# Key transfers of an attention kernel issued from ScalarE's queue instead of SyncE's

## The chip, the core and the metric

The kernel runs on one core of a Trainium2 chip. The time is the device time of one execution in microseconds (us). The core has five engines, each of which takes its own instructions in order: PE (TensorE), DVE (VectorE), ACT (ScalarE), POOL (GpSimd) and SP (SyncE, which here only issues transfers). They meet at semaphores. 16 DMA engines do the transfers; an engine's queue only issues them.

## The reference

Eight images of 32 x 32 tokens go through one transformer layer of width 128: an embedding with a position table, causal attention with 8 heads of 16, and a feed-forward block with a shared and 8 routed experts of which each token takes 2. Cut to what matters here:

```python
h = x @ W + pe                                    # (8, 1024, 128)
z = layernorm(h)
Q, K, V = (split_heads(z @ w + b) for w, b in ((Wq, bq), (Wk, bk), (Wv, bv)))
attn = softmax((Q @ K.T + causal_mask) / sqrt(16))
h = h + (attn @ V) @ Wo + bo
f = layernorm_with_scale(layernorm(h))
h = h + shared_expert(f) + sum_over_top2(weight[e] * expert[e](f))
```

Everything is float32. The products that need it are made of three passes with split operands: a high part (`_h`) and the rest (`_l`).

## The kernel before, in words

An image has 1024 tokens, worked on in two halves of 512. Its heads are taken in two groups of four, so the attention has four units, a group and a half of the queries each. For an image the steps are, in their names in the code: `emb`, `turn1`, `q`, `k`, `v` for each half (embedding, normalisation, transposed tokens, the two projections and the values); 64 `score` steps, first pass, which find the largest score of every query; 96 `prob` steps in 24 groups of four, second pass, in which PE makes transposed scores in one of two banks, ACT takes their exponential into `pt`, and `weigh` multiplies by the values; then the projection (`to`, `ant`, `oproj`), the second normalisation, routing (`gates`, `route`), and the feed-forward steps `in`, `expert`, `shared`, `counts` and `combine`.

**The stacks.** Both passes of scores multiply `q_stack` by `k_stack`. In each, three copies of a head's 16 rows lie below each other (high, high, low for the queries; high, low, high for the keys), with the even heads' copies in partitions 0 to 47 and the odd heads' from partition 64. The copies are made by DMA within the core's memory: six transfers of 128 KB for the queries of a half and six for its keys. What is copied are `qk_h`, which ACT writes straight from the projection (L953), and `qk_l`, which POOL subtracts (L1101). `stack_in[half]` counts the twelve transfers; PE waits for all of them before `score 0` of an image (half 0) and before `score 32` (half 1).

**Order.** A table (`PERIOD`) lists all steps of one period in one order, and every engine walks through it and does its own part of each step. In a period the second pass and the feed-forward part of image i are woven with the front (`emb` to `v`) and the first half of the scores of image i+1. `FIRST` is the same front for image 0, and `LAST` is the rest for image 7, so seven periods hold a front of a next image. The keys of half 0 may be overwritten once the last probability step that reads them is through (`KEYS_USED`, the 20th group of 24); until then SP's `keys` waits. All transfers of the loop are issued by SP.

Since each engine takes its instructions in order, an instruction that waits, or one that takes long to issue, holds everything behind it on that engine.

Of the kernel before, what the change touches and what calls it, by code (L numbers as in the profile page):

```python
# [36 lines left out]
P = 128  # L37
# [4 lines left out]
HEADS, DH = 8, 16  # L42
G4 = 4
# [7 lines left out]
ODD = 64  # L51
# [12 lines left out]
NS, NP_, NU = len(SCORE_STEPS), len(PROB_STEPS), len(UNITS)  # L64
# [3 lines left out]
KEYS_USED = max(k for k, (_, kt) in enumerate(PROB_STEPS) if kt < HT)  # L68
# [10 lines left out]
def later(i):  # L79

    return not (isinstance(i, int) and i == 0)
# [15 lines left out]
def of_next_image(st):  # L97

    return (st[0] in ("emb", "turn1", "q", "k", "v") or st[0] == "score" and st[1] < 2 * UNIT_S or
            st[0] == "turn" and st[1] < 2)  # L100
# [49 lines left out]
PERIOD = period(WEAVE, streams())  # L150
# [14 lines left out]
def build(nc, x_t, tok_w, pos, wq, wk, wv, wo, bq, bk, bv, bo, ln_s, ln_b, w_in, w_shared, w_expert, w_bias,  # L165
          w_gate, b_gate, out):
    with ExitStack() as ctx:
# [3 lines left out]
        def sem(name):  # L171
            return ctx.enter_context(nc.semaphore(name))
# [36 lines left out]
        qk_h, qk_l = sb("qk_h", [P, 2, S], F32R), sb("qk_l", [P, 2, S], F32R)  # L209
        v = sb("v", [P, TILES, HEADS, VW])  # L210

        q_stack = sb("q_stack", [P, 2, HEADS, HALF], F32R)
        k_stack = sb("k_stack", [P, HEADS // 2, S], F32R)
# [55 lines left out]
        front_mm = sem("front_mm")  # L269
# [9 lines left out]
        qkh_made, qkl_made = sem("qkh_made"), sem("qkl_made")  # L279
        v_made = sem("v_made")  # L280
        stack_in = [sem(f"stack_in_{half}") for half in range(2)]
# [4 lines left out]
        st_ready, exp_done, mask_done = sem("st_ready"), sem("exp_done"), sem("mask_done")  # L286
# [18 lines left out]
        stacks_zeroed = sem("stacks_zeroed")  # L305
# [4 lines left out]
        def halfs(half):  # L310
            return slice(half * HALF, (half + 1) * HALF)
# [4 lines left out]
        def front_step(i, what, half):  # L316

            return i * NF + FRONT_STEPS.index((what, half)) + 1
# [5 lines left out]
        def words(ap):  # L324

            return ap.bitcast(F32)
# [4 lines left out]
        @block.sync  # L331
        def _(sp):
            def load_x(i):
                sp.dma_start(x_sb[:], x_t[:, bass.ds(i * S, S)]).then_inc(x_in, 16)

            load_x(0)
            for dst, src in ((tokw_sb, tok_w), (pos_sb, pos)):
                sp.dma_start(dst[:], src).then_inc(w_in0, 16)
            for dst, src in ((wq_sb, wq), (wk_sb, wk), (bq_sb, bq), (bk_sb, bk),
                             (wv_sb, wv), (bv_sb, bv), (bo_sb, bo)):  # L340
                sp.dma_start(dst[:], src).then_inc(w_in1, 16)
            for dst, src in ((wo_sb, wo), (lns_sb, ln_s), (lnb_sb, ln_b), (win_sb, w_in), (wshared_sb, w_shared),
                             (wex_sb, w_expert), (wbias_sb, w_bias), (wgate_sb, w_gate), (bgate_sb, b_gate)):
                sp.dma_start(dst if dst is win_sb or dst is wex_sb else dst[:], src).then_inc(w_in2, 16)

            sp.wait_ge(const_made, CONSTS)
            sp.wait_ge(stacks_zeroed, 3)
            for n in range(HEADS // 2):
                sp.dma_start(words(k_stack[SHIFT:P, n, :]), words(minus1.rearrange("r c n -> r (c n)"))).then_inc(ones_in, 16)

            def stacks(i, half, w):

                if w == 0:
                    sp.wait_ge(qkh_made, i * 4 + 2 * half + 2)
                    sp.wait_ge(qkl_made, i * 4 + 2 * half + 2)
                for n, part in enumerate((qk_h, (qk_h, qk_l)[w], (qk_l, qk_h)[w])):
                    for odd in range(2):
                        to = slice(odd * ODD + n * DH, odd * ODD + (n + 1) * DH)
                        stack = k_stack[to, :, halfs(half)] if w else q_stack[to, half, odd::2, :]
                        rows = part[odd * (P // 2):(odd + 1) * (P // 2), w, halfs(half)]  # L360
                        sp.dma_start(words(stack), words(rows)).then_inc(stack_in[half], 16)  # L361

            def maxima(i, u):

                g, half = UNITS[u]
                sp.wait_ge(ml_made, i * NU + u + 1)
                for row, part in ((SHIFT, mrow_h), (SHIFT + 1, mrow_l)):
                    dst = q_stack[row:row + 1, half, g * G4:(g + 1) * G4, :]
                    sp.dma_start(words(dst), words(part[:, u, :])).then_inc(m_in[u], 16)

            def store(i, half):
                sp.wait_ge(ex_step, (i * TILES + (half + 1) * HT) * COMBINE)
                sp.dma_start(out_v[i, :, tiles(half), :], acc[:, tiles(half), :]).then_inc(out_done[half], 16)

            def stage(i, st, loads=True):
                if st[0] == "turn":
                    maxima(i, st[1])
                elif st == ("k", 0):
                    stacks(i, 0, 0)
                    if not later(i):  # L380
                        stacks(i, 0, 1)
                elif st == ("k", 1):
                    stacks(i, 1, 0)
                    stacks(i, 1, 1)
                    if loads:
                        load_x(i + 1)
                elif st == ("combine", 3):
                    store(i, 0)
                elif st == ("combine", 7):
                    store(i, 1)  # L390

            def keys(i):

                sp.wait_ge(exp_done, i * NP_ * G4 + (KEYS_USED + 1) * G4)
                stacks(i + 1, 0, 1)

            def image(i, loads):
                for n, st in enumerate(PERIOD):
                    stage(i + of_next_image(st), st, loads)
                    if n == max(PERIOD.index(("k", 0)), PERIOD.index(("prob", KEYS_USED, G4 - 1))):  # L400
                        keys(i)

            for st in FIRST:
                stage(0, st)
            image(0, True)
            for i in range(1, B - 2):
                image(i, True)
            image(B - 2, False)
            for st in LAST:
                stage(B - 1, st)  # L410
            for half in range(2):
                sp.wait_ge(out_done[half], B * 16)
# [525 lines left out]
        def _(act):  # L938
            def front(i, kind, half):
                if kind == "turn1":  # L940
                    if later(i):
                        act.wait_ge(z2l_made, i * 2 - 1 + half)
                    act.wait_ge(front_mm, front_step(i, "turn1", half))
                    src = (b7, b6)[half]
                    nc.scalar.copy(zt[:, halfs(half)], src[:]).then_inc(zt_made, 1)
                    nc.scalar.copy(zt_h[:, halfs(half)], src[:]).then_inc(zth_made, 1)
                if kind in ("q", "k"):
                    w = "qk".index(kind)
                    src, bias = (b6 if half and w else b7), (bq_sb, bk_sb)[w]
                    act.wait_ge(front_mm, front_step(i, kind, half))  # L950
                    nc.scalar.activation(qk[:, w, halfs(half)], src[:], ACT.Identity,
                                         bias=bias[:, 0:1]).then_inc(qk_made, 1)
                    nc.scalar.activation(qk_h[:, w, halfs(half)], src[:], ACT.Identity,  # L953
                                         bias=bias[:, 0:1]).then_inc(qkh_made, 1)

            def take(i, u):

                g, half = UNITS[u]
                act.wait_ge(pv_done, i * NP_ + UNIT_LAST[u] + 1)
                nc.scalar.copy(ot[:, g, halfs(half)], b6[:]).then_inc(pv_taken, 1)  # L960
# [69 lines left out]
            def stage(i, st):  # L1030
                if st[0] == "prob":
                    prob(i, st[1], st[2])
                elif st[0] == "take":
                    take(i, st[1])
                elif st[0] in ("turn1", "q", "k"):
                    front(i, st[0], st[1])
                elif st[0] in ("in", "counts", "expert", "combine"):
                    forward(i, st)
                elif st[0] in ("ant", "z2t", "route"):
                    post(i, st)  # L1040

            def image(i):
                for st in PERIOD:
                    stage(i + of_next_image(st), st)

            act.wait_ge(w_in1, 7 * 16)
            for st in FIRST:
                stage(0, st)
            act.wait_ge(w_in2, 9 * 16)
            nc.scalar.copy(win_h[:], win_sb).then_inc(wsplit_h, 1)  # L1050
            nc.scalar.copy(wex_h[:], wex_sb).then_inc(wsplit_h, 1)
# [189 lines left out]
```

## Time and profile before

| | |
|---|---|
| Time, 3 runs | 1180.1 us median (1179.13 to 1182.12) |
| The profiled execution | 1181.4 us, its span 1179.6 us |
| PE busy | 1063.7 us, 90% of the span |
| DVE / ACT / POOL busy | 64% / 53% / 33% |
| Granted TensorE clock, mean | 0.938 of full speed |
| Share of PE in the chain that ended last | 75% |
| Share of the transfers and SP's issues in that chain | 6% and 5% |

A period takes about 139.9 us: the last key transfer of half 0 was issued at 430.75 us in one and at 570.64 us in the next. The times of a row are microseconds from the start of the span. "Idle before" is the time in which the engine had nothing to execute, with the instruction that ended it. In the views by stretch, PEclk 1.00 is the full TensorE clock of 2.4 GHz and 0.50 is 1.2 GHz; a value between them means that the clock changed within the stretch.

### The profile page before, as it was taken

The page shows a single profiled execution, that of the slowest core. Times are in us where ns is not written, and L with a number is a line of the kernel's source. Part 1 is how long each engine was busy: PE and PEld are TensorE (multiplying, and loading weights), DVE is VectorE, ACT ScalarE, POOL GpSimd, SP SyncE. Part 2 cuts the span into 40 slices and gives each one's busy share as a digit, 9 for nine tenths or more (in the row PEclk, how much of TensorE's full clock was granted, in tenths as well). Part 3 has the DMA queues.
Part 4 walks back from the last instruction along what each step waited for, and adds up shares of the span by engine and source line. Part 5 has one row for each costly group of instructions (what it writes and reads, how often), then busy time and mean ns, then how long its engine had stood idle before and what let it go on. Part 6 is the DMA issues. An engine that isn't in the chain of part 4 may idle for free.

```text
span 1179.6 us, 16622 instructions
## 1 busy us (share of the span) xinstructions
PE 1063.7 (90%) x5632; PEld 706.6 (60%) x5632; DVE 756.8 (64%) x2118; ACT 628.9 (53%) x1395; POOL 388.0 (33%) x514
## 2 busy tenths in 40 slices
PE   2589988999799988999889998899979998899997
PEld 1345566556675566755666556755667556675575
DVE  3387558874678537785387755787377854778444
ACT  1226825567346654567345672556734665446743
POOL 5321424313432234412353142432333223441233
PEclk9969988999899998999889998899989999899999
DMA  3530032103040040400404003310304004040000
GB/s 96 70 43 1 16 40 50 29 2 48 8 67 11 2 54 10 68 1 2 54 20 58 2 17 39 54 24 1 51 8 64 11 2 54 10 64 1 1 1 18
DMA packets 28547, 34.60 MB, mean 29 GB/s; under 512 B 5402, under 2 KB 15552, under 8 KB 28336
## 3 DMA queue, kind: packets, MB, share of 16 engines
q1 hardware_dynamic: 28464, 33.55, 18.3%
q8 instruction: 45, 0.74, 0.3%
q14 instruction: 38, 0.31, 0.1%
HBM read 3.61 MB, written 4.19 MB: 7 GB/s over the span
## 4 chain that ended last, share of the span: by engine, by line
PE 75%; DVE 7%; DMA 6%; SPq 5%; ACT 4%; issue 2%; POOL 1%; DVEq 0%; POOLq 0%; ACTq 0%
PE bank L517 15%; PE bank L536 12%; PE pair L488 9%; PE bank L488 5%; DMA k_stack<-qk_h 5%; PE pair L656 5%; PE pair L657 5%; PE pair L658 5%; SPq L361 5%; ACT pt L969 2%; PE pair L419 2%; PE pair L420 2%; PE pair L421 2%; PE bank L637 2%; PE bank L431 1%
## 5 line engine op out<-in xcount | busy, mean ns | idle before, releaser
L969 ACT ACTIVATE pt<-bank 128x512 f32<-128x512 f32 (+3 forms) x768 | 346.6, 493 | 211.6 <-PE bank L517 204.3
L741 DVE CUSTOM_DVE_ANT_0 pair<-pair,causal 128x640 f32<-128x640 f32 (+3 forms) x256 | 257.2, 1047 | 36.9 <-PE pair L488 34.8
L517 PE MATMUL bank<-q_stack,k_stack 128*128 128x512 f32 (+2 forms) x768 | 266.2, 399 | 9.2 <-ACT pt L969 7.3
L517 PEld LDWEIGHTS bank<-q_stack,k_stack 128*128 128x128 f32 x768 | 135.6, 190 | 165.1 <-ACT pt L969 126.3
L1113 POOL TENSOR_SCALAR_AFFINE_SELECT pt<-pt 128x512 f32<-128x512 f32 x128 | 81.7, 638 | 364.5 <-ACT pt L969 364.5
L536 PE MATMUL bank<-pt,v 128*32 128x512 f32 (+3 forms) x1536 | 168.9, 513 | 2.1 <-ACT pt L969 2.1
L741 DVE CUSTOM_DVE_ANT_0 bank<-bank,causal 128x128 f32<-128x128 f32 (+3 forms) x256 | 121.9, 509 | 61.1 <-PE bank L488 60.7
L488 PE MATMUL pair<-k_stack,q_stack 112*128 112x512 f32 (+2 forms) x512 | 148.8, 380 | 7.4 <-issue 6.2
L488 PE MATMUL bank<-k_stack,q_stack 112*128 112x256 f32 (+2 forms) x256 | 90.1, 424 | 29.1 <-DMA k_stack<-qk_h 22.7
L488 PEld LDWEIGHTS pair<-k_stack,q_stack 112*128 112x128 f32 x512 | 86.2, 191 | 44.8 <-DVE mx L741 28.8
L656 PE MATMUL pair<-wex_h,hid_h 128*128 128x512 f32 x256 | 106.9, 418 | 0.6 <-POOL hid_l L1136 0.4
L1015 ACT ACTIVATE from_act<-pair,gm 128x512 f32<-128x512 f32 x64 | 44.1, 689 | 113.3 <-PE pair L658 105.0
L657 PE MATMUL pair<-wex_l,hid_h 128*128 128x512 f32 x256 | 104.4, 408 | 0.0
L658 PE MATMUL pair<-wex_h,hid_l 128*128 128x512 f32 x256 | 104.1, 407 | 0.0
L1144 POOL TENSOR_TENSOR from_dve<-from_act 128x256 f32<-128x256 f32 x64 | 46.7, 730 | 171.9 <-ACT from_act L1021 171.2
L1021 ACT ACTIVATE from_act<-from_dve,wsel 128x128 f32<-128x128 f32 x256 | 81.7, 391 | 35.9 <-DVE from_dve L893 35.4
L488 PEld LDWEIGHTS bank<-k_stack,q_stack 112*128 112x128 f32 x256 | 52.3, 228 | 50.5 <-DMA k_stack<-qk_h 26.5
L893 DVE SCALAR_TENSOR_TENSOR from_dve<-pair,gm,from_act 128x512 f32<-128x512 f32 x64 | 47.8, 747 | 50.9 <-PE pair L658 47.5
L866 DVE SCALAR_TENSOR_TENSOR from_dve<-from_act,pair 128x512 f32<-128x512 f32 x64 | 43.9, 685 | 47.4 <-PE pair L421 43.9
L741 DVE DVE_READ_ACCUMULATOR2_ANT mx<- 128x1 f32 x512 | 72.2, 141 | 0.0
L419 PE MATMUL pair<-z2t_h,win_h 128*128 128x512 f32 x128 | 59.1, 462 | 2.0 <-issue 1.8
L658 PEld LDWEIGHTS pair<-wex_h,hid_l 128*128 128x128 f32 x256 | 50.2, 196 | 12.6
(142 smaller groups left out, 1537.6 us busy)
## 6 DMA issues: line engine op xcount, KB each, us to landing
q_stack<-qk_h SPq DMA_DIRECT2D x64, 128.0 KB, 4.0
k_stack<-qk_h SPq DMA_DIRECT2D x64, 128.0 KB, 6.5
q_stack<-qk_l SPq DMA_DIRECT2D x32, 128.0 KB, 5.0
k_stack<-qk_l SPq DMA_DIRECT2D x32, 128.0 KB, 6.7
out<-h SPq DMA_DIRECT2D x16, 256.0 KB, 2.3
pt<-w_expert SPq DMA_DIRECT2D x1, 1024.0 KB
x_sb<-x_t SPq DMA_DIRECT2D x8, 116.0 KB
pos_sb<-pos SPq DMA_DIRECT2D x1, 512.0 KB
```

The costliest lines, as they stand in the source:

```text
L361: sp.dma_start(words(stack), words(rows)).then_inc(stack_in[half], 16)
L419: nc.tensor.matmul(dst, wh, xh, start=first, stop=False)
L488: mm = nc.tensor.matmul(dst[:, a:b], q_stack[0:STACK, t // HT, hd, t % HT * P:(t % HT + 1) * P], k_stack[0:STACK, hd // 2, a:b], start=Tru ...
L517: nc.tensor.matmul((b4, b5)[p % 2][:, c0:HALF], k_stack[:, hd // 2, kt * P:(kt + 1) * P], q_stack[:, half, hd, c0:HALF], start=True, stop= ...
L536: mm = nc.tensor.matmul(b6[32 * j:32 * j + VW, q0:HALF], v[:, kt, g * G4 + j, :], pt[:, k % PT_SLOTS, j, q0:HALF], start=(kt == 0), stop=( ...
L656: nc.tensor.matmul(dst, hid_h[:, c, tok], wex_h[:, c, w], start=(c == 0), stop=False)
L657: nc.tensor.matmul(dst, hid_h[:, c, tok], wex_l[:, c, w], start=False, stop=False)
L658: mm = nc.tensor.matmul(dst, hid_l[:, c, tok], wex_h[:, c, w], start=False, stop=(c == HID // P - 1))
L741: nc.vector.tensor_tensor_reduce(src, src, causal[:, S - n:S], 1.0, -3.0e38, ALU.add, ALU.max, mx[:, col:col + 1]).then_inc(s_taken, 1)
L969: nc.scalar.activation(pt[:, k % PT_SLOTS, j, q0:HALF], (b4, b5)[p % 2][:, q0:HALF], ACT.Exp, scale=0.25).then_inc(exp_done, 1)
L1021: nc.scalar.mul(from_act[:, t % 2, part], from_dve[:, t % 2, part], wsel[:, t, e:e + 1]).then_inc(weighted, 1)
L1113: nc.gpsimd.affine_select(out=d, in_=d, compare_op=ALU.is_ge, fill=0.0, base=0, pattern=[[0, G4], [1, P]], channel_multiplier=-1).then_inc ...
```

## The change

The six transfers of the keys of a half move from SP's queue to ACT's. On SP stay those of the queries, and their wait changes: they no longer wait for the keys' parts to be made, only for the queries' own. On ACT a function `keys` waits for the keys' parts (both of ACT's and POOL's), and for image 1 and later also until PE is through with the keys that are overwritten, then issues six transfers. For half 0 that stands after the step at place 161 of the table (`in 3`, second part), for half 1 in the step `("v", 1)`, which ACT had nothing to do in. SP's load of the next image's tokens gets a wait of its own. The diff, whole:

```diff
--- before.py
+++ after.py
@@ -348,17 +348,17 @@
             for n in range(HEADS // 2):
                 sp.dma_start(words(k_stack[SHIFT:P, n, :]), words(minus1.rearrange("r c n -> r (c n)"))).then_inc(ones_in, 16)
 
-            def stacks(i, half, w):
-
-                if w == 0:
-                    sp.wait_ge(qkh_made, i * 4 + 2 * half + 2)
-                    sp.wait_ge(qkl_made, i * 4 + 2 * half + 2)
-                for n, part in enumerate((qk_h, (qk_h, qk_l)[w], (qk_l, qk_h)[w])):
+            def queries(i, half):
+
+                sp.wait_ge(qkh_made, i * 4 + 2 * half + 1)
+                sp.wait_ge(qkl_made, i * 4 + 2 * half + 1)
+                if half and later(i):
+                    sp.wait_ge(st_ready, i * NP_ * G4)
+                for n, part in enumerate((qk_h, qk_h, qk_l)):
                     for odd in range(2):
                         to = slice(odd * ODD + n * DH, odd * ODD + (n + 1) * DH)
-                        stack = k_stack[to, :, halfs(half)] if w else q_stack[to, half, odd::2, :]
-                        rows = part[odd * (P // 2):(odd + 1) * (P // 2), w, halfs(half)]
-                        sp.dma_start(words(stack), words(rows)).then_inc(stack_in[half], 16)
+                        rows = part[odd * (P // 2):(odd + 1) * (P // 2), 0, halfs(half)]
+                        sp.dma_start(words(q_stack[to, half, odd::2, :]), words(rows)).then_inc(stack_in[half], 16)
 
             def maxima(i, u):
 
@@ -376,29 +376,20 @@
                 if st[0] == "turn":
                     maxima(i, st[1])
                 elif st == ("k", 0):
-                    stacks(i, 0, 0)
-                    if not later(i):
-                        stacks(i, 0, 1)
+                    queries(i, 0)
                 elif st == ("k", 1):
-                    stacks(i, 1, 0)
-                    stacks(i, 1, 1)
+                    queries(i, 1)
                     if loads:
+                        sp.wait_ge(front_mm, front_step(i, "emb", 1))
                         load_x(i + 1)
                 elif st == ("combine", 3):
                     store(i, 0)
                 elif st == ("combine", 7):
                     store(i, 1)
 
-            def keys(i):
-
-                sp.wait_ge(exp_done, i * NP_ * G4 + (KEYS_USED + 1) * G4)
-                stacks(i + 1, 0, 1)
-
             def image(i, loads):
-                for n, st in enumerate(PERIOD):
+                for st in PERIOD:
                     stage(i + of_next_image(st), st, loads)
-                    if n == max(PERIOD.index(("k", 0)), PERIOD.index(("prob", KEYS_USED, G4 - 1))):
-                        keys(i)
 
             for st in FIRST:
                 stage(0, st)
@@ -953,6 +944,20 @@
                     nc.scalar.activation(qk_h[:, w, halfs(half)], src[:], ACT.Identity,
                                          bias=bias[:, 0:1]).then_inc(qkh_made, 1)
 
+            def keys(i, half):
+
+                act.wait_ge(qkh_made, i * 4 + 2 * half + 2)
+                act.wait_ge(qkl_made, i * 4 + 2 * half + 2)
+                if not later(i):
+                    act.wait_ge(stacks_zeroed, 3)
+                if later(i):
+                    act.wait_ge(st_ready, (i - 1) * NP_ * G4 + (NP_ if half else KEYS_USED + 1) * G4)
+                for n, part in enumerate((qk_h, qk_l, qk_h)):
+                    for odd in range(2):
+                        to = slice(odd * ODD + n * DH, odd * ODD + (n + 1) * DH)
+                        rows = part[odd * (P // 2):(odd + 1) * (P // 2), 1, halfs(half)]
+                        act.dma_start(words(k_stack[to, :, halfs(half)]), words(rows)).then_inc(stack_in[half], 16)
+
             def take(i, u):
 
                 g, half = UNITS[u]
@@ -1034,18 +1039,24 @@
                     take(i, st[1])
                 elif st[0] in ("turn1", "q", "k"):
                     front(i, st[0], st[1])
+                elif st == ("v", 1):
+                    keys(i, 1)
                 elif st[0] in ("in", "counts", "expert", "combine"):
                     forward(i, st)
                 elif st[0] in ("ant", "z2t", "route"):
                     post(i, st)
 
             def image(i):
-                for st in PERIOD:
+                for n, st in enumerate(PERIOD):
                     stage(i + of_next_image(st), st)
+                    if n == max(PERIOD.index(("k", 0)) + 6, PERIOD.index(("prob", KEYS_USED, G4 - 1))):
+                        keys(i + 1, 0)
 
             act.wait_ge(w_in1, 7 * 16)
             for st in FIRST:
                 stage(0, st)
+                if st == ("k", 0):
+                    keys(0, 0)
             act.wait_ge(w_in2, 9 * 16)
             nc.scalar.copy(win_h[:], win_sb).then_inc(wsplit_h, 1)
             nc.scalar.copy(wex_h[:], wex_sb).then_inc(wsplit_h, 1)
```

ACT's instructions in the first period around half 0, in the order of its program (an ACTIVATE of `pt` is the exponential of one probability step, `from_act<-pair` on L996 is the tanh of an `in` step, L1028 the copy of the counts; square brackets name the semaphores waited for). Before:

```order
L996 ACTIVATE from_act<-pair 128x512 [waits in_ready]
L969 ACTIVATE pt<-bank 128x512 [waits st_ready]
L969 ACTIVATE pt<-bank 128x384 [waits st_ready,pv_done]
L1004 CAST hid_h<-hid 128x512 [waits hid_made]
L996 ACTIVATE from_act<-pair 128x512 [waits in_ready]
L969 ACTIVATE pt<-bank 128x384 [waits st_ready] x2
L1028 COPY cnt_t<-bank 9x512 [waits cnt_ready]
L969 ACTIVATE pt<-bank 128x384 [waits st_ready]
```

After (the same instructions have other line numbers there: L996 is L1001, L969 is L974, L1004 is L1009, L1028 is L1033; L959 is the new issue):

```order
L1001 ACTIVATE from_act<-pair 128x512 [waits in_ready]
L974 ACTIVATE pt<-bank 128x512 [waits st_ready]
L974 ACTIVATE pt<-bank 128x384 [waits st_ready,pv_done]
L1009 CAST hid_h<-hid 128x512 [waits hid_made]
L1001 ACTIVATE from_act<-pair 128x512 [waits in_ready]
L959 DMA k_stack<-qk_h 16x4x512 [waits st_ready,qkl_made,qkh_made]
L959 DMA k_stack<-qk_h 16x4x512
L959 DMA k_stack<-qk_l 16x4x512 x2
L959 DMA k_stack<-qk_h 16x4x512 x2
L974 ACTIVATE pt<-bank 128x384 [waits st_ready] x2
L1033 COPY cnt_t<-bank 9x512 [waits cnt_ready]
L974 ACTIVATE pt<-bank 128x384 [waits st_ready]
```

Six transfers now stand between the first and the second exponential of the group that works on 384 columns. Later in the same period, around half 1 (L951 and L953 write the keys' projection, L996 is the tanh of the last `in` step, L1015 an expert's selection), ACT before:

```order
L1004 CAST hid_h<-hid 128x512 [waits ex_ready,hid_made]
L951 ACTIVATE ot<-bank,bk_sb 128x512 [waits front_mm]
L953 ACTIVATE qk_h<-bank,bk_sb 128x512
L996 ACTIVATE from_act<-pair 128x512 [waits in_ready]
L1015 ACTIVATE from_act<-pair,gm 128x512 [waits route_step,ex_ready]
L1015 ACTIVATE from_act<-pair,gm 128x512 [waits ex_ready]
```

After (L951, L953 and L1015 are L942, L944 and L1020):

```order
L1009 CAST hid_h<-hid 128x512 [waits ex_ready,hid_made]
L942 ACTIVATE ot<-bank,bk_sb 128x512 [waits front_mm]
L944 ACTIVATE qk_h<-bank,bk_sb 128x512
L959 DMA k_stack<-qk_h 16x4x512 [waits st_ready,qkl_made,qkh_made]
L959 DMA k_stack<-qk_h 16x4x512
L959 DMA k_stack<-qk_l 16x4x512 x2
L959 DMA k_stack<-qk_h 16x4x512 x2
L1001 ACTIVATE from_act<-pair 128x512 [waits in_ready]
L1020 ACTIVATE from_act<-pair,gm 128x512 [waits route_step,ex_ready]
L1020 ACTIVATE from_act<-pair,gm 128x512 [waits ex_ready]
```

The wait for POOL's part of the keys (`qkl_made`) and the six transfers now stand between the keys' projection and the tanh.

## Rows read from the trace of the kernel before

**Rows 1.** The page: busy time, share of the span and instructions of each engine.
```profile
PE 1063.7 (90%) x5632; PEld 706.6 (60%) x5632; DVE 756.8 (64%) x2118; ACT 628.9 (53%) x1395; POOL 388.0 (33%) x514
```
**Rows 2.** Waits of PE: for whom, us in total, times, longest us.
```profile
PE bank L488 <- DMA k_stack<-qk_h: 22.7, 8, 6.2
```
**Rows 3.** Timeline, half 0: start us, us, engine, line, operation, count, idle before.
```profile
419.32 1.30 POOL L1101 TENSOR_TENSOR qk_l<-ot,qk_h 128x512 fp32r<-128x512 f32 x1 [2.84 <-ACT qk_h L953]
422.32 1.29 POOL L1101 TENSOR_TENSOR qk_l<-ot,qk_h 128x512 fp32r<-128x512 f32 x1 [0.45 <-ACT qk_h L953]
423.69 2.52 SPq L361 DMA_DIRECT2D q_stack<-qk_h  x4
435.27 0.64 PE L536 MATMUL bank<-pt,v 128*32 128x256 f32 x8
438.36 0.50 PE L488 MATMUL bank<-k_stack,q_stack 112*128 112x256 f32 x2 [2.45 <-DMA k_stack<-qk_h]
```
**Rows 4.** Stretches: length, busy PE, PEld, DVE, ACT, POOL, PEclk, DMA share, GB/s.
```profile
432.00:436.00 4.00, 3.60 (x30) 2.04 (x29) 1.31 (x2) 1.28 (x5) 1.80 (x3) 1.00 1.06 124
438.40:439.00 0.60, 0.60 (x6) 0.46 (x10) 0.21 (x1) 0.00 (x0) 0.00 (x0) 0.79 0.00 0
445.00:446.00 1.00, 1.00 (x7) 0.77 (x6) 0.02 (x1) 0.00 (x0) 0.00 (x0) 0.71 0.00 0
463.00:464.00 1.00, 0.00 (x0) 0.00 (x0) 1.00 (x3) 0.58 (x2) 0.67 (x2) 0.50 0.00 0
469.00:470.00 1.00, 1.00 (x5) 0.82 (x5) 0.74 (x3) 0.97 (x2) 0.00 (x0) 0.76 0.00 0
```
**Rows 5.** Timeline of PE: the same product at half and full clock; two other pauses.
```profile
444.45 0.63 PE L656 MATMUL pair<-wex_h,hid_h 128*128 128x512 f32 x1
444.88 0.63 PE L657 MATMUL pair<-wex_l,hid_h 128*128 128x512 f32 x1
446.46 0.40 PE L656 MATMUL pair<-wex_h,hid_h 128*128 128x512 f32 x1
446.69 0.39 PE L657 MATMUL pair<-wex_l,hid_h 128*128 128x512 f32 x1
464.40 1.12 PE L440 MATMUL bank<-ident,z 128*128 128x128 f32 x4 [3.16 <-DVE z L717]
494.55 0.94 PE L488 MATMUL pair<-k_stack,q_stack 112*128 112x512 f32 x4 [0.88 <-issue]
```
**Rows 6.** SP's issues: duration ns min/median/max, first and last start; one other issue.
```profile
L361 SPq DMA_DIRECT2D k_stack<-qk_h x64: 592/600/1550, 35.9 to 1043.4; - x64
463.78 0.38 SPq L373 DMA_DIRECT2D out<-h  x1
```
**Rows 7.** Timeline of ACT and PE at the place of half 0's new issues.
```profile
424.46 0.91 ACT L969 ACTIVATE pt<-bank 128x384 f32<-128x384 f32 x2
425.84 0.56 PE L517 MATMUL bank<-q_stack,k_stack 128*128 128x384 f32 x2
```
**Rows 8.** Timeline, half 1: POOL, ACT, DVE and PE around the new issues.
```profile
472.12 1.29 POOL L1101 TENSOR_TENSOR qk_l<-ot,qk_h 128x512 fp32r<-128x512 f32 x1 [0.61 <-ACT qk_h L953]
474.61 1.30 POOL L1101 TENSOR_TENSOR qk_l<-ot,qk_h 128x512 fp32r<-128x512 f32 x1
474.69 0.60 ACT L996 ACTIVATE from_act<-pair 128x512 f32<-128x512 f32 x1 [0.32 <-PE pair L421]
475.90 0.68 DVE L866 SCALAR_TENSOR_TENSOR from_dve<-from_act,pair 128x512 f32<-128x512 f32 x1
477.22 0.29 DVE L741 CUSTOM_DVE_ANT_0 bank<-bank,causal 128x128 f32<-128x128 f32 x1
478.33 0.40 PE L488 MATMUL bank<-k_stack,q_stack 112*128 112x256 f32 x2
```
**Rows 9.** Timeline of the front of image 0 (POOL's queries' part, and SP).
```profile
27.57 1.27 POOL L1101 TENSOR_TENSOR qk_l<-ot,qk_h 128x512 fp32r<-128x512 f32 x1 [3.08 <-ACT qk_h L953]
31.98 2.58 SPq L361 DMA_DIRECT2D q_stack<-qk_h  x4
```

## The prediction

> **What bounds the kernel now.** I read the page's busy times first: PE is busy for 90% of the span and the next engine for 64% [rows 1]. A microsecond in which PE stands still inside a period is therefore a microsecond of the result, unless PE would have stood still a little later anyway. Next I read PE's waits for the transfers that the change touches. There is one entry: the first score of an image waited 8 times for the last key transfer, 22.7 us in total, the longest 6.2 us [rows 2]. The longest is image 0; the other seven share 16.5 us, 2.36 us each. The third view is the timeline around one of them. POOL has the queries' low part ready at 419.32 + 1.30 = 420.62 and the keys' at 422.32 + 1.29 = 423.61. SP issues nothing before 423.69, then twelve transfers, and PE starts score 0 at 438.36 after 2.45 us of idling [rows 3]. From the first issue to the use are 14.67 us. Half 1 has no such wait: all eight entries belong to score 0.
>
> The fourth view is the granted clock. After that pause it falls from 1.00 within the stretch 438.40 to 439.00, at about 438.65 (0.79 is 58% of a level of 0.5 and 1), wait included or not, and comes back within 445.00 to 446.00, at about 445.6 [rows 4]. So some 6.9 us run at 1.2 GHz, and there the same product starts every 0.43 us instead of every 0.23 us [rows 5]. Lost: 6.9 x (1 - 0.23/0.43) = 3.2 us, of which I count 2.9 us, since PE alternates with DVE in part of it. The pause of 3.16 us before 464.40 does the same, but there the clock is already at 0.50 in the stretch 463 to 464 and returns by about 469.5, so that 5.1 us of work run at half speed: 2.4 us lost [rows 4, 5]. A pause of 0.88 us before 494.55 ends in a product at the full rate, four in 0.94 us [rows 5]. A pause of two to four microseconds thus costs about two and a half more in the clock, one below a microsecond does not.
>
> **What the change takes away.** SP's half-0 issues shrink from twelve to six and start when the queries' part is ready, 3.0 us earlier than now (420.7 for 423.69). All twelve transfers still go through the same 16 DMA engines, and these are full while the keys are under way: their share is 1.06 in the stretch 432 to 436, at 124 GB/s [rows 4]. So the twelve need their 14.6 us from the first issue whoever issues them, and the last lands at about 420.7 + 14.6 = 435.3. PE was ready for it at 438.36 - 2.45 = 435.91. The wait of 2.36 us goes, by a margin of 0.6 us, and with it its clock loss. In image 0 the issue moves from 31.98 to 27.57 + 1.27 + 0.05 = 28.9 [rows 9], and the wait there is 6.2 us, so 3.1 us are gained, once. For half 1 nothing is gained, because nobody waits there.
>
> **What it adds.** ACT now issues six transfers in the stream of its own instructions, twice per period. The trace before has no issue by ACT. The nearest rows are the same transfers on SP: 600 ns each, and with the step between them 0.64 us, so six take 3.86 us. The cheapest issue of SP in the loop is 0.38 us, the longest of these 1.55 us [rows 6]. I take 0.64 us and keep 0.38 and, from the side of a gain, an issue that holds ACT for nothing. Above, 1.55 us for all six would be 9.3 us; it was the longest of 64, so it is an end and no more.
>
> *Half 0.* The six stand before the exponential that started at 424.46. It starts at 424.46 + 3.86 = 428.32 instead. PE's next probability product but one waits for that exponential, nearly 0.5 us long, because there are two banks; it started at 425.84 [rows 7] and now starts at about 428.85, and its neighbour, which needs the second exponential, 3.1 us later than now. PE takes its instructions in order, so the experts' products behind are late too. All other waits that the keys' landing could make are hidden: PE arrives at score 0 at 435.9 + 3.1 = 439.0, well behind 435.3. A pause of 3 us costs its clock loss as well, about what the removed one cost. Net per period: +3.1 - 2.36, clock against clock, = +0.7 us.
>
> *Half 1.* ACT waits for POOL's keys' part, ready at 474.61 + 1.30 = 475.91, issues from 475.98 to 479.84, and only then does the tanh that ran at 474.69 [rows 8]. It ends at 480.44. DVE's gate follows at 480.5, and DVE also takes in order: the score that it reads behind the two gate operations began 1.32 us after the first of them (475.90 to 477.22), so at 481.8, and its maximum is out 0.35 us later. PE has two banks of scores and needs that before the pair that it started at 478.33 [rows 8]; it gets it at 482.2. That is 3.9 us of standing still in a stretch where PE was fully busy, and it is followed by no pause that could absorb it but the 0.88 us at 494.55, which comes from an expert's result that is late by the same amount. The clock: a pause of 3.9 us is like the one of 3.16 us, 2.4 us lost. Per period +6.3 us.
>
> **The sum.** (0.7 + 6.3) x 7 periods - 3.1 = +45.9 us. The profiled execution was 1181.4 us, 1.3 us above the median of the runs, so 1227.3 against it and 1226 against the median of 1180.1.
>
> One rule speaks for the change. The Trainium skill, "Perfetto Trace Analysis", section "DMA Optimizations", says that when descriptor generation is the bottleneck, seen as an issuer that looks busy with slices, spreading transfers over the issuing engines may help. SP does look like that here, and if only delivery counted, the gain would be the first rival's below. The section says nothing of what stands behind the issues on the new queue, and that is where my sum has its large term. Another page ("DMA: Bandwidth & Descriptors", section "Issuing engines are not separate DMA queues") says that spreading only saves the sequencer's time, usually small relative to the DMA. Ratio and rule agree (0.6 us for each issue), but six in a row are not small beside ACT's 0.5 us exponentials.
>
> **Rivals.**
> - *ACT is not held.* If an issue costs ACT some 0.1 us, half 0 keeps its gain, 2.36 + 2.9 = 5.3 us, less 0.3; in half 1 the tanh is late, but there are some 0.7 us between the maximum at 477.22 + 0.35 = 477.6 and its use at 478.33, so about +0.5 remains. -4.5 x 7 - 3.1 = -35: 1145 us. For it: no row shows an issue on ACT, and nothing says that it must cost what it costs on SP. Against it: the same issues on SP cost 0.6 us in the median and never less than 0.59 [rows 6], with nothing else for SP to do, so the time seems to be the issue's own. The side changes where six issues take about 2 us: below that the half-0 pause is under a microsecond and keeps the clock.
> - *Cheap but not free, 0.38 us.* Six take 2.3 us. Half 0: a pause of 1.4 us for one of 2.36 us, perhaps without the clock loss: -1.0 to -3.9. Half 1: a pause of 2.3 us and 2.4 of clock: +4.7. Sum +0.8 to +3.7 per period, 1183 to 1203.
> - *The clock stays up through the new pauses.* Half 0 then gains 2.9 us of clock, half 1 costs 3.9 only: +1.7 x 7 - 3.1 = +9, 1189. Against it: pauses of 2.4 and 3.2 us lowered it. If only half 1's is spared, 1209.
> - *The two queues hold each other up.* In half 1, SP issues its six from 472.12 + 1.29 + 0.1 = 473.5 to 477.3 [rows 8], over ACT's first two. If those double, +1.3 x 7 = +9, 1235. If every issue of ACT's takes 0.75 us, both pauses grow by 0.7 us: 1236; both together 1245.
>
> **Chances and range.** The forecast with its own variations (1209 to 1246) has 0.67, an issue that does not hold ACT 0.16, the cheap issue or the spared clock (1183 to 1203) 0.12, worse than 1246 0.05. A measurement of this kernel tells 0.3%, some 3.5 us, from no change. Faster by more than that: 0.17, from the first rival and the cheapest end of the second; within it 0.05; slower 0.78. The range leaves out most of the first rival and the top: 1165 to 1246. The likeliest case alone: 1209 to 1246.
>
> **What would show it.** In the profile after: issues on ACT's queue of 0.6 us each, 96 in all; PE's wait for the key transfer gone except in image 0, where it is about 3 us; in its place PE idle for about 3 us before a probability product that waits for ACT, and for about 4 us before a score that waits for DVE's maximum, once each per period; the clock at half after both. The period grows from 139.9 to about 147 us. The forecast is wrong if the issues on ACT are short, if the tanh between them and the experts turns out not to hold DVE's scores, or if the wait for the keys remains.

## The result, and the profile after

| | before | changed |
|---|---|---|
| Median of the runs | 1180.11 us (1179.13 to 1182.12) | 1204.07 us (1200.38 to 1206.73) |
| Ratio, 95% interval | | 1.0199 (1.0162 to 1.0235) |
| Profiled execution, its span | 1181.4, 1179.6 us | 1206.73, 1205.0 us |
| Mean granted clock | 0.938 | 0.950 |

Slower by 24 us, as forecast in sign; 46 us were forecast. The interval excludes no change, and leaves open whether the loss is above or below 2%. The page of the changed kernel, against [rows 1]: PE has the same work, and its share fell because the span grew. In the chain that ended last ACT's queue rose from 0% to 2%, SP's queue (5% before) is gone, and the transfers' share fell from 6% to 1%.

```profile
PE 1065.2 (88%) x5632; PEld 701.8 (58%) x5632; DVE 757.2 (63%) x2118; ACT 627.8 (52%) x1395; POOL 387.0 (32%) x514
...
PE 74%; DVE 7%; issue 6%; ACT 5%; ACTq 2%; POOL 2%; DMA 1%; DVEq 0%; POOLq 0%
```

What PE waited for in the changed kernel (in total, times, longest). The wait of [rows 2] is left in image 0 alone. In its place stand two entries. The kernel before had 5.6 us for the first of them and 7.3 us for the second.

```profile
PE bank L479 <- DVE mx L732: 31.7, 28, 4.7
PE bank L508 <- ACT pt L974: 22.9, 24, 2.6
...
PE bank L479 <- DMA k_stack<-qk_h: 3.5, 1, 3.5
```

The issues on ACT's queue (duration in ns, min/median/max), against those on SP in [rows 6]:

```profile
L959 ACTq DMA_DIRECT2D k_stack<-qk_h x64: 554/620/1451, 31.9 to 1060.5; - x64
L959 ACTq DMA_DIRECT2D k_stack<-qk_l x32: 615/622/1549, 33.3 to 1059.2; - x32
```

The long ones are rare. In the last half-1 batch one stood beside slow issues of SP's (two of 0.6 us each would be 1.2):

```profile
1056.50 2.91 SPq L361 DMA_DIRECT2D q_stack<-qk_l  x2
1056.46 2.04 ACTq L959 DMA_DIRECT2D k_stack<-qk_h  x2
```

Timeline of the changed kernel around half 0, the same period as [rows 3, 7]: ACT executes nothing between the end of the tanh and 433.32, then the held exponential, and PE's product follows after 2.60 us of idling.

```profile
429.05 0.57 ACTq L959 DMA_DIRECT2D k_stack<-qk_h  x1
429.32 0.64 ACT L1001 ACTIVATE from_act<-pair 128x512 f32<-128x512 f32 x1
...
432.01 1.27 ACTq L959 DMA_DIRECT2D k_stack<-qk_h  x2
433.32 0.87 ACT L974 ACTIVATE pt<-bank 128x384 f32<-128x384 f32 x2 [3.37 <-issue]
433.87 0.77 PE L508 MATMUL bank<-q_stack,k_stack 128*128 128x384 f32 x2 [2.60 <-ACT pt L974]
```

Around half 1, against [rows 8]: the issues end at 483.58, then come the tanh, DVE's gate, DVE's maximum and PE's score, each released by the one before. This is the chain of the prediction, link by link.

```profile
479.54 1.21 ACTq L959 DMA_DIRECT2D k_stack<-qk_h  x2
480.78 1.50 ACTq L959 DMA_DIRECT2D k_stack<-qk_l  x2
482.31 1.27 ACTq L959 DMA_DIRECT2D k_stack<-qk_h  x2
483.63 0.60 ACT L1001 ACTIVATE from_act<-pair 128x512 f32<-128x512 f32 x1 [5.69 <-issue]
...
484.31 0.69 DVE L857 SCALAR_TENSOR_TENSOR from_dve<-from_act,pair 128x512 f32<-128x512 f32 x1 [4.71 <-issue]
485.64 0.29 DVE L732 CUSTOM_DVE_ANT_0 bank<-bank,causal 128x128 f32<-128x128 f32 x1
...
486.04 0.77 PE L479 MATMUL bank<-k_stack,q_stack 112*128 112x256 f32 x2 [3.95 <-DVE mx L732]
```

**Where the 25.4 us of span went.** Both programs issue the same 5632 products in the same order, so the start of each can be set against the start of the same one before. The difference jumps at few places:

| place | jumps in the seven periods, us | sum |
|---|---|---|
| image 0, score 0 | -2.7 | -2.7 |
| half 0, product behind the held exponential | 2.2, 2.5, 2.7, 2.4, 2.2, 2.3, 2.3 | +16.5 |
| score 0, the old wait | -2.5, -2.3, -2.5, -2.5, -2.3, -2.3, -2.5 | -17.0 |
| half 1, score behind the held tanh | 4.9, 4.1, 4.1, 3.0, 3.0, 3.0, 4.8 | +26.9 |
| everything between, nearly all of it the clock | | +1.7 |

That it is the clock is read from where the slips stand: where its level differs between the two traces. The last line is made of +11.7 from half 0's new pause to score 0 (0.2 in three periods, 1.8, 5.9, 1.8 and 1.6 in four), -17.3 from score 0 to the half-1 place, where the old clock loss is gone, and +7.3 from there on. Behind the 3.95 us pause shown, the clock was at half for 3.4 us (0.92 of 3 us and a third of 2 us):

```profile
487.00:490.00 3.00, 3.00 (x12) 2.16 (x11) 0.76 (x5) 0.91 (x2) 0.00 (x0) 0.54 1.05 124
490.00:492.00 2.00, 2.00 (x9) 1.69 (x9) 1.00 (x4) 1.54 (x5) 0.39 (x1) 0.83 0.23 34
```

### The profile page after: what moved, and what is told of

It reads as the page before. It is cut to its first block, busy times and chain, and to the rows that moved or that the text cites. A ratio compares the mean times of both kernels' runs of the same rounds, so it can differ in the third digit from the quotient of the medians.

```text
span 1205.0 us, 16638 instructions
## 1 busy us (share of the span) xinstructions
PE 1065.2 (88%) x5632; PEld 701.8 (58%) x5632; DVE 757.2 (63%) x2118; ACT 627.8 (52%) x1395; POOL 387.0 (32%) x514
## 4 chain that ended last, share of the span: by engine, by line
PE 74%; DVE 7%; issue 6%; ACT 5%; ACTq 2%; POOL 2%; DMA 1%; DVEq 0%; POOLq 0%
PE bank L508 16%; PE bank L527 12%; PE pair L479 9%; PE bank L479 5%; PE pair L647 5%; PE pair L649 4%; PE pair L648 4%; PE bank L628 3%; ACT pt L974 3%; ACTq L959 2%; PE bank L629 2%; PE pair L410 1%; PE pair L411 1%; PE pair L412 1%; PE bank L422 1%
## 5 line engine op out<-in xcount | busy, mean ns | idle before, releaser
L974 ACT ACTIVATE pt<-bank 128x512 f32<-128x512 f32 (+3 forms) x768 | 346.3, 492 | 225.0 <-PE bank L508 196.2
L508 PE MATMUL bank<-q_stack,k_stack 128*128 128x512 f32 (+2 forms) x768 | 269.0, 401 | 24.8 <-ACT pt L974 22.9
L527 PE MATMUL bank<-pt,v 128*32 128x512 f32 (+3 forms) x1536 | 165.6, 503 | 2.1 <-ACT pt L974 2.1
L1020 ACT ACTIVATE from_act<-pair,gm 128x512 f32<-128x512 f32 x64 | 44.0, 687 | 119.1 <-PE pair L649 110.7
L869 DVE TENSOR_TENSOR h<-bank,h 128x512 f32<-128x512 f32 x16 | 11.1, 691 | 94.0 <-PE bank L629 94.0
L1001 ACT ACTIVATE from_act<-pair 128x512 f32<-128x512 f32 x64 | 38.9, 607 | 58.1 <-issue 41.2
```

The source lines that it names most:

```text
L508: nc.tensor.matmul((b4, b5)[p % 2][:, c0:HALF], k_stack[:, hd // 2, kt * P:(kt + 1) * P], q_stack[:, half, hd, c0:HALF], start=True, stop= ...
L527: mm = nc.tensor.matmul(b6[32 * j:32 * j + VW, q0:HALF], v[:, kt, g * G4 + j, :], pt[:, k % PT_SLOTS, j, q0:HALF], start=(kt == 0), stop=( ...
L974: nc.scalar.activation(pt[:, k % PT_SLOTS, j, q0:HALF], (b4, b5)[p % 2][:, q0:HALF], ACT.Exp, scale=0.25).then_inc(exp_done, 1)
```

## The experiments

Theory A: six issues in a row hold ACT for as long as they take, PE ends up waiting behind them, and a second queue delivers nothing earlier. The rivals stand in the expectations. Each kernel is compared with runs of before on the same chip (1181.04 us for the first four, 1180.04 us for the last three).

**Half 1 alone, and half 0 alone.** The first keeps SP's code of before for half 0:

```diff
                 elif st == ("k", 0):
-                    queries(i, 0)
+                    stacks(i, 0, 0)
+                    if not later(i):
+                        stacks(i, 0, 1)
...
+            def keys(i):
+                sp.wait_ge(exp_done, i * NP_ * G4 + (KEYS_USED + 1) * G4)
+                stacks(i + 1, 0, 1)
...
-                    if n == max(PERIOD.index(("k", 0)) + 6, PERIOD.index(("prob", KEYS_USED, G4 - 1))):
-                        keys(i + 1, 0)
```

> Only the keys of half 1 are issued by ACT; half 0 is as in the kernel before. Theory A (six issues hold ACT, PE waits behind them; the clock follows the pauses): the changed kernel's half-1 pauses, 26.9 us in all, stay, with their clock loss, and nothing of half 0's gain comes back, so slower than the changed kernel, about 1210 to 1215 us; PE's wait for the key transfers is back at 22.7 us. Rival B (the loss comes from the two queues getting in each other's way on the DMA engines, so that transfers land late): both halves add to it, and this one alone costs about half, 1190 us.

1215.65 us, ratio 1.0289 (1.0271 to 1.0306). The jumps at the half-1 place are 4.9, 4.2, 4.2, 4.9, 4.1, 4.2, 4.6 us, and PE's wait for the key transfers is back at 22.5 us. The pauses sum to 31.0 us, 4.1 more than in the changed kernel. The time is Theory A's (just above its 1215), and far from B's 1190, so B is out. The second experiment keeps SP's `stacks` for half 1 and leaves out ACT's in `("v", 1)`:

```diff
                 elif st == ("k", 1):
-                    queries(i, 1)
+                    stacks(i, 1, 0)
+                    stacks(i, 1, 1)
...
-                elif st == ("v", 1):
-                    keys(i, 1)
```

> Only the keys of half 0 are issued by ACT; half 1 is as in the kernel before. Theory A: one pause of 2.3 us for another of 2.4 us in each period, 2.7 us less in image 0, and the clock falls less often, so faster than before by 5 to 10 us, about 1172 us; before + (this - before) + (half 1 only - before) gives the changed kernel within 4 us. Rival B: half of the loss, 1190 us.

1154.90 us, ratio 0.9779 (0.9764 to 0.9793): faster than before by 26 us, far more than I expected. So the half-0 part of the change is a gain and the half-1 part is all of the loss. The pauses are those of the changed kernel, 2.3 to 2.7 us, but the clock stood through six of the seven; its mean is 0.976. All its jumps together give -3.4 us; the other 23 us lie between them, and added up from the trace's clock, PE was at half for 147 us in the kernel before, 120 us in the changed one and 55 us here. That is where more was gained than the 5 to 10 us expected. The additive sum fails as well, by 14.6 us where I had allowed 4: 1181.0 + 34.6 - 26.1 = 1189.5 us against 1204.1. A half-0 pause of this kernel, and two stretches at and behind it (length, busy PE, PEld, DVE, ACT, POOL, clock, DMA share, GB/s):

```profile
556.70 0.77 PE L520 MATMUL bank<-q_stack,k_stack 128*128 128x384 f32 x2 [2.19 <-ACT pt L986]
```

```profile
555.00:560.00 5.00, 3.30 (x17) 2.59 (x18) 0.00 (x0) 3.17 (x8) 0.64 (x1) 1.00 1.08 118
560.00:566.00 6.00, 5.69 (x37) 4.01 (x38) 0.69 (x1) 1.41 (x6) 0.74 (x2) 1.00 0.44 52
```

And the changed kernel at and behind the pause of the same line, one period on:

```profile
717.65 0.76 PE L508 MATMUL bank<-q_stack,k_stack 128*128 128x384 f32 x2 [2.17 <-ACT pt L974]
```

```profile
720.00:724.00 4.00, 4.00 (x16) 3.10 (x14) 0.00 (x0) 1.23 (x3) 0.00 (x0) 0.50 0.96 113
724.00:730.00 6.00, 6.00 (x23) 3.64 (x23) 0.69 (x1) 0.38 (x1) 0.63 (x1) 0.50 0.00 0
```

The first kernel's pause of 2.19 us ended in full clock; the second's of 2.17 us was followed by 13.7 us at 1.2 GHz (719.4 to 733.1), in which PE was busy nearly all the time. The length of a pause and the instructions around it don't settle what the clock does.

**Only the early queries.** Everything stays on SP; the queries' transfers wait for the queries' parts alone:

```diff
-                if w == 0:
-                    sp.wait_ge(qkh_made, i * 4 + 2 * half + 2)
-                    sp.wait_ge(qkl_made, i * 4 + 2 * half + 2)
+                sp.wait_ge(qkh_made, i * 4 + 2 * half + w + 1)
+                sp.wait_ge(qkl_made, i * 4 + 2 * half + w + 1)
...
                 elif st == ("k", 1):
+                    if later(i):
+                        sp.wait_ge(st_ready, i * NP_ * G4)
```

The wait added before half 1 stands in the changed kernel's `queries` too: it keeps the stacks from being overwritten before PE has made the last probability scores of the image before.

> All twelve transfers stay on SP, but those of the queries no longer wait for the keys' parts. Nothing on ACT. Theory A: the twelve start 3.0 us earlier and land at 435.3 where PE needs them at 435.9, so the 16.5 us of PE's waits in seven periods go, with 3.1 us in image 0 and the clock loss after the old pauses (2.4 us each), together 36 us: about 1144 us. Theory C (a second queue is needed for the keys to land earlier, because SP's own issue rate bounds them): most of the wait remains, 1175 us or more.

1138.33 us, ratio 0.9641 (0.9626 to 0.9655), the fastest kernel of all here, and 6 us below Theory A's 1144. PE's wait for the transfers is left in image 0 alone, and nothing replaces it:

```profile
PE bank L518 <- ACT pt L970: 7.3, 17, 0.8
PE bank L489 <- DVE mx L742: 6.2, 22, 0.9
...
PE bank L489 <- DMA k_stack<-qk_h: 3.1, 1, 3.1
```

In one period, the first and the last of SP's issues and PE's score 0 without a pause:

```profile
406.09 2.52 SPq L360 DMA_DIRECT2D q_stack<-qk_h  x4
413.26 1.25 SPq L360 DMA_DIRECT2D k_stack<-qk_h  x2
421.25 0.51 PE L489 MATMUL bank<-k_stack,q_stack 112*128 112x256 f32 x2
```

The stretches in which the transfers end (the last two columns are the DMA share and GB/s), and the last issue with its time to landing, that is until its semaphore is up:

```profile
413.00:417.00 4.00, 4.00 (x26) 3.11 (x25) 0.00 (x0) 1.24 (x3) 0.00 (x0) 1.00 1.07 129
417.00:419.00 2.00, 1.99 (x14) 0.91 (x13) 0.69 (x1) 0.41 (x2) 0.63 (x1) 1.00 0.92 110
419.00:421.00 2.00, 1.70 (x18) 1.41 (x18) 0.22 (x1) 0.86 (x4) 0.76 (x2) 1.00 0.02 2
```

```profile
413.90 0.61 SPq L360 DMA_DIRECT2D k_stack<-qk_h  x1
DMA to landing us min/median/max: 6.5/6.5/6.5
```

The DMA engines are full to the end and nearly idle from 419, some 13 us after the first issue. The landing that PE waits for comes later than that, at 413.90 + 6.5 = 420.4, which is 14.3 us after the first issue and 0.9 us before PE's score 0; in the other six periods it is 0.5 to 0.6 us. The kernel before shows the same delay: its DMA engines were idle from 437 on while PE still waited until 438.36.

```profile
437.00:438.00 1.00, 0.00 (x0) 0.00 (x0) 0.00 (x0) 0.00 (x0) 0.00 (x0) 1.00 0.00 0
```

One queue is enough; what counted was when the first of the twelve starts. That rules out theory C. All kernels here with half 0's keys on ACT have this early start too, so it and not the second queue is their gain: half 0 alone is 16.6 us slower than this kernel, and its seven half-0 pauses sum to 16.4 us (that the two agree so well is partly luck, as its clock was at half for 55 us and here for 73).

**Half 1's keys later in ACT's stream.** As the changed kernel, but:

```diff
-                elif st == ("v", 1):
-                    keys(i, 1)
...
+                    if st == ("combine", 5):
+                        keys(i + 1, 1)
```

> As the changed kernel, but ACT issues the keys of half 1 behind the weights of combine 5, where ACT stood idle for over 4 us (483.17 + 1.28 to 488.76 in the trace before). Theory A: no tanh, no DVE and no PE behind it is held, the half-1 pauses and their clock loss go, about 1172 us, unless the keys now land after 493.7 us of that period's time, where PE would wait for stack_in; that wait would be below 2 us per period. Rival B: the transfers are as many on as many queues, so 1204 us as the changed kernel.

1160.88 us, ratio 0.9828 (0.9787 to 0.9870), so faster, though not surely by 2%, and 11 us below the 1172 expected. The four runs spread from 1154.8 to 1165.4 us, with a mean clock of 0.970 in the fastest and 0.957 in the slowest, which is the one traced. For image 0 the issues keep their place. The jump at the half-1 place is gone in all periods, with the same transfers on the same two queues; B is out. ACT issues while it would idle, and the instruction behind still waits 4.32 us for PE, as it did before:

```profile
481.75 0.55 ACTq L959 DMA_DIRECT2D k_stack<-qk_h  x1
...
484.29 1.27 ACTq L959 DMA_DIRECT2D k_stack<-qk_h  x2
487.26 0.69 ACT L1020 ACTIVATE from_act<-pair,gm 128x512 f32<-128x512 f32 x1 [4.32 <-PE pair L649]
```

**Six tiny transfers.** The kernel before, and on ACT in the step `("v", 1)`:

```diff
+            def held(i):
+                act.wait_ge(const_made, 1)
+                act.wait_ge(scratch_in, i * 96)
+                for n in range(6):
+                    act.dma_start(scratch[0:16, n * TILES:(n + 1) * TILES], half_pow[0:16, :]).then_inc(scratch_in, 16)
```

> The kernel before, all its transfers on SP, and on ACT in the step (v, 1) of every image six transfers of 512 bytes each between two tiles that nothing else uses, with no wait for POOL. Theory A (what holds ACT is the issue itself, whatever is moved): each issue takes 0.5 to 0.6 us as the 8 KB ones on SP do, ACT starts the tanh about 3.3 us later than it finished the keys' projection, 474.36 + 3.3 = 477.7 for 474.69; PE's half-1 pause is about 1.8 us in each period, with some clock loss: 1195 us. Rival D (ACT is held by the 128 KB moving, through a full queue): the tiny ones cost 0.1 us and nothing shows, 1181 us.

1174.29 us, ratio 0.9943 (0.9913 to 0.9972). (What the expectation calls the 8 KB issues are those of the 128 KB transfers, 8 KB for each of 16 partitions.) The issues cost what those of 128 KB cost, which rules out D, and hold the tanh in the same way. The issues' durations, and the timeline of ACT around half 1:

```profile
L962 ACTq DMA_DIRECT2D scratch<-half_pow x48: 514/611/1260, 51.9 to 1036.2; - x48
```

```profile
473.80 0.68 ACT L955 ACTIVATE qk_h<-bank,bk_sb 128x512 fp32r<-128x512 f32 x1
473.82 3.17 ACTq L962 DMA_DIRECT2D scratch<-half_pow  x5
477.04 0.60 ACT L1004 ACTIVATE from_act<-pair 128x512 f32<-128x512 f32 x1 [2.56 <-issue]
```

But the time missed my 1195 us by 21 us. The jumps are 1.0 to 1.7 us, 8.1 us in all, not 1.8 each, since the issues start before ACT has executed what stands ahead of them; and the kernel is nevertheless 0.6% faster than before in the median of ten runs. These spread from 1163.5 us (mean clock 0.972) to 1180.9 us (0.948); the one traced is the slowest and as long as the kernel before, with its 8.1 us of jumps made up by the clock. The kernel before had its clock at half in this stretch of six of its periods, and this one of one. Before first, then this (length, busy time of the five engines, clock, DMA share, GB/s):

```profile
544.00:548.00 4.00, 4.00 (x23) 1.93 (x23) 1.32 (x8) 3.71 (x7) 1.28 (x2) 0.57 0.00 0
```

```profile
544.00:548.00 4.00, 3.49 (x23) 1.74 (x26) 2.95 (x13) 3.36 (x7) 2.74 (x4) 1.00 0.00 0
548.00:552.00 4.00, 4.00 (x28) 1.86 (x20) 1.56 (x10) 3.67 (x7) 1.28 (x1) 1.00 0.00 0
```

In the traced run a shift of a microsecond in a period went with a change in the clock that was worth slightly more than the shift. Whether the one caused the other is not shown beyond this pair of kernels.

**The wait for POOL alone.**

```diff
+            def held(i):
+                act.wait_ge(qkl_made, i * 4 + 4)
```

> The kernel before with one more wait on ACT in the step (v, 1): for POOL's low part of the keys, and no transfer. The tanh moves from 474.69 to 475.95, DVE's maximum from 477.57 to about 478.3, just where PE takes it at 478.33. Theory A: no change, 1181 us, within 2 us; the wait alone is hidden and only the issues behind it are not. Rival E (the wait for POOL is half of the matter): a half-1 pause of above 1 us, 1190 us or more.

1179.90 us, ratio 0.9996 (0.9985 to 1.0008), and no jump at the half-1 place. ACT does wait, 1.57 us in the row below, and nobody behind it notices. E is out.

```profile
473.26 0.60 ACT L999 ACTIVATE from_act<-pair 128x512 f32<-128x512 f32 x1 [1.57 <-POOL qk_l L1106]
```

**Three issues for six.** As the changed kernel, but in half 1 ACT loops over `range(half, 2)` in place of `range(2)`, and SP does the even heads' keys behind the queries.

> As the changed kernel, but in half 1 ACT issues only the three transfers of the odd heads and SP the other three behind the queries. Theory A: ACT is held for 2 us instead of 4, the half-1 pause falls from 3.0 to 4.8 us to 1.5 to 2.5 us, 14 us less in seven periods before the clock: 1204 - 14 = 1190 us, within 8 us for the clock. Rival B (it is the mixture on the DMA engines): as the changed kernel, 1204 us.

1177.90 us, ratio 0.9981 (0.9968 to 0.9994). The jumps at the half-1 place are 2.0, 2.3, 1.9, 1.9 and 1.9 us in five periods, 3.2 us in one, and in one 1.8 us spread over three products, 15 us in all against 26.9: the hold scales with the number of issues. The time is far from B's 1204, 12 us below my 1190, and outside the 8 us I allowed for the clock, whose mean is 0.961 here.

## Why the prediction was right, and where it was off

- **The wait removed.** Predicted 16.5 us in seven periods and 3.1 us in image 0; measured 17.0 and 2.7 us. That the twelve transfers, starting 3 us earlier, land in time was right, and so was the margin of 0.6 us: with everything on SP it is 0.5 to 0.9 us.
- **The cost of an issue on ACT**, unseen in the trace before and taken from SP: 0.64 us predicted with its step, 0.62 us in the median measured plus the step, with single ones up to 1.55 us. Six took 4.0 us in the half-1 row shown, against 3.86. The rivals of an issue that is free or costs 0.38 us are out. Two of the seven half-1 batches had one issue of 1.55 or 1.45 us, took 4.7 us, and have pauses of 4.9 and 4.8 us. In the one shown SP's issues were slow at the same time, which is what the rival of the two queues holding each other up says; it was worth under 1 us each time.
- **Half 0's pause.** Predicted 3.1 us, measured 2.2 to 2.7 us. I let the six begin with the start of the held exponential; the first began before ACT had even started the tanh ahead of it (429.05 and 429.32), so the queue ran ahead of the engine.
- **Half 1's pause.** Predicted 3.9 us by seven, 27.3; measured 26.9. The single ones are 3.0 to 4.9 us, so that the sum fits this well is partly luck; with half 1 alone they sum to 31.0 us.
- **The clock: the term that was mis-sized.** The prediction said of half 0 that a pause of 3 us "costs its clock loss as well, about what the removed one cost", and of half 1 "2.4 us lost". That made 0 and +16.8 us. Measured: +11.7 behind the new half-0 pauses, -17.3 from score 0 to the half-1 place and +7.3 from there on, +1.7 in all. These 15.1 us, with 5.4 us of half 0's jumps (+4.9 forecast, -0.5 measured), are the difference between the 45.9 us forecast and the 25.4 us by which the span grew.
- **Half 0's part of it.** The loss removed was sized rightly: behind score 0 the starts gain 2.6 to 2.7 us in each period, here and in the kernel with only the early queries, where I had counted 2.9. But the clock fell behind only four of the seven new pauses.
- **Half 1's part of it.** Within 8 us behind the new pause the starts slip by 1.9, 1.9, 1.9, 1.6, 1.6, 3.1 and 1.9 us, 14.0 in all, so the 16.8 was nearly right: the clock fell behind all seven, for 3.4 us in six of them, where I had counted 5.1 us of work at half speed. The other 6.7 us come from a place that the prediction did not look at. The kernel before has a third fall of the clock, 3.4 us long, in six of its periods, and the changed kernel has it in two; four of these falls and one of 6.8 us at 1145.3 are gone behind the half-1 places. It also speaks against the prediction's rule that a pause below a microsecond does not cost the clock: the longest within 8 us ahead of this fall, at 404.6, is 0.51 us.

```profile
403.51 0.99 PE L517 MATMUL bank<-q_stack,k_stack 128*128 128x512 f32 x2 [0.51 <-ACT pt L969]
```

```profile
404.00:408.00 4.00, 4.00 (x24) 1.99 (x23) 1.38 (x8) 3.64 (x7) 1.28 (x2) 0.58 0.00 0
```

- The rival "the clock stays up through the new pauses" (1189 us if through all) came true in three of seven half-0 pauses and in none of half 1. It was given too little weight. The result lies between it and the forecast, 5 us below the 1209 to 1246 us that had the chance of 0.67. The pauses were predicted to a few microseconds, and what the clock makes of them was not. The period grew from 139.7 to 143.9 us on average, not to 147.
- One reading is off by 0.1 us: a mean of 0.79 over 438.40 to 439.00 puts the fall at 438.75, not 438.65, so the half clock lasts 6.8 us.

Open: why the same half-0 pause lowered the clock in four of seven periods of the changed kernel and in one of seven with half 0 alone on ACT. The instructions around it are the same. I did not find what decides it, so a forecast of this kernel by its pauses alone is uncertain by some 15 us, the misfit of the sum above.

## What to carry to other kernels

Moving a transfer to a computing engine's queue costs that engine the issue, here 0.6 us each for 512 bytes as for 128 KB, in the order of its stream; put it where the engine waits for something anyway, or not there at all. Before a second queue is tried, look at what the first transfer of the batch waits for: here it waited for data that it doesn't copy, and dropping that wait gave more (-42.7 us) than any of the divisions over two queues tried, which had it dropped as well. When a forecast rests on the clock's answer to a pause, give each pause a cost between zero and the largest seen, and widen the range accordingly.

## What the runs showed of the hardware that I had not expected

- An issue on ACT takes 0.61 us in the median for 512 bytes and 0.62 us for 128 KB.
- PE took up its work over 1.3 us after the 16 DMA engines had gone idle (438.36 and 437.0 us in the kernel before): the last transfer's landing is not the end of the DMA's busy time.
- A half-0 pause of 2.2 to 2.7 us was followed by no half-clock time, by 3.4 us or by 13.7 us of it, in the same kernel.
- Eight microseconds of added pauses left the traced run as long as before (spans of 1179.2 and 1179.6 us); a fall of the clock elsewhere in the period came once instead of six times. Ten runs of that same kernel spread over 17 us, with mean clocks of 0.948 to 0.972.
- In the kernel before the clock fell at 404.6 us with no pause above 0.51 us in the 8 us ahead of it.
- Effects that went through the clock did not add: the two halves of the change apart give 1189.5 us, together 1204.1 us.
